# Constant loads at the head of SP's queue, block loads moved next to their use, and the mask moved from slot 28 to slot 10

## The reference

```python
x = x + tanh(g_xattn[0]) * L0_xattn(layernorm(x), ...)
x = x + tanh(g_ffn[0]) * L0_ffn(layernorm(x), ...)          # stage B and the start of stage C
x = x + tanh(g_xattn[1]) * L1_xattn(layernorm(x), ctx, ctx, mask, Wq, bq, ..., Wo, bo)
x = x + tanh(g_ffn[1]) * L1_ffn(layernorm(x), w1, conv_w, conv_b, w2)

# L0_ffn: per-tensor quantised activations, per-row quantised weights, inner width 1408
xq   = act_fake_quant(x, clip_x)                 # scale, clip to -128..127, round
gate = xq @ weight_fake_quant(w_gate).T
up   = xq @ weight_fake_quant(w_up).T
h    = act_fake_quant(silu(gate) * up, clip_down)   # needs the largest |silu(gate)*up| of all tokens
y    = h @ weight_fake_quant(w_down).T
# L1_ffn quantises w1 and w2 to -1, 0, 1 with the mean of their absolute values as scale
```

## Time and profile before

| | us |
|---|---|
| median of 3 runs | 1983.57 (1983.23 to 1985.07) |
| the profiled execution, its own time | 1985.07 |
| its span | 1983.3 |
| stage B in it | about 975 to 1158 |

### The profile page before, as it was taken

The page is one execution under the profiler, slowest core; times in us unless marked ns, Lnnn a source line. Parts: engine busy times, 40 slices in busy tenths (PEclk is TensorE's granted clock), DMA queues, the critical chain, the costliest instruction groups (busy, mean ns, idle before and its releaser), DMA issues.

```text
span 1983.3 us, 24380 instructions
## 1 busy us (share of the span) xinstructions
PE 1599.7 (81%) x9442; PEld 718.8 (36%) x9510; DVE 1743.9 (88%) x2619; ACT 1485.4 (75%) x1098; POOL 616.9 (31%) x480
## 2 busy tenths in 40 slices
PE   6858966698557966785599969999999976888887
PEld 3212211122112211231244426666666632334432
DVE  6899998999999987898598877999998669999997
ACT  4899999999999999999354845554554357767771
POOL 1000000000000000000062236666666446887881
PEclk9999999999999999999799989999999988999998
DMA  5000200020000010000387753333332110432312
GB/s 199 1 0 29 79 11 1 22 75 22 1 1 1 22 54 1 1 11 1 110 312 291 265 172 100 112 112 112 107 100 81 43 37 27 79 61 70 57 43 74
DMA packets 116710, 143.66 MB, mean 72 GB/s; under 512 B 25327, under 2 KB 74607, under 8 KB 116211
## 3 DMA queue, kind: packets, MB, share of 16 engines
q1 hardware_dynamic: 116594, 142.10, 22.9%
HBM read 87.55 MB, written 50.33 MB: 70 GB/s over the span
## 4 chain that ended last, share of the span: by engine, by line
ACT 43%; PE 30%; DVE 19%; issue 4%; POOL 3%; DMA 2%; SPq 0%; DVEq 0%; another core or an unknown queue 0%; POOLq 0%; ACTq 0%
ACT unit L514 39%; PE psum L1647 5%; PE psum L1681 5%; PE psum L1633 3%; DVE hmax_parts L1429 3%; DVE psum L1418 3%; PE psum L1016 3%; PE psum L1010 3%; DVE unit L423 2%; PE psum L1657 2%; PE psum L1674 2%; POOL hidden L1837 1%; PE psum L1666 1%; PE psum L547 1%; DVE hidden_q L1453 1%
## 5 line engine op out<-in xcount | busy, mean ns | idle before, releaser
L514 ACT ACTIVATE unit<-unit 128x4096 f32<-128x4096 f32 x244 | 857.6, 3620 | 0.5 <-DVE unit L423 0.3
L423 DVE TENSOR_SCALAR unit<-feat_proj,text_proj 128x1024 f32<-128x1024 f32 x976 | 667.5, 747 | 67.2 <-PE psum L639 65.2
L639 PE MATMUL psum<-unit,w_pad 128*32 128x512 f32 x3904 | 474.8, 605 | 234.1 <-ACT unit L514 234.1
L639 PEld LDWEIGHTS psum<-unit,w_pad 128*32 128x32 f32 x3904 | 102.5, 109 | 557.3 <-ACT unit L514 398.6
L680 POOL TENSOR_SCALAR red<-red 128x8 f32<-128x8 f32 x4 | 2.0, 510 | 531.5 <-DVE red L321 531.5
L1820 POOL TENSOR_TENSOR h<-h,arow 128x512 f32<-128x512 f32 x104 | 135.7, 1318 | 73.0 <-ACT h L1582 72.8
L1699 PE MATMUL psum<-xq_block,w_q 128*128 128x512 bf16 x489 | 122.8, 391 | 27.5 <-ACT hidden L1601 21.3
L680 POOL TENSOR_SCALAR rstd<-mv 128x8 f32<-128x8 f32 (+1 forms) x5 | 1.7, 336 | 411.7 <-DVE mv L216 411.7
L547 PE MATMUL psum<-xnT,W_sb 128*128 128x512 f32 x256 | 125.2, 617 | 2.1 <-ACT xnT L465 2.1
L1589 ACT ACTIVATE psum<-h,conv_b_sb,conv_w_sb 128x512 f32<-128x512 f32 x112 | 86.2, 779 | 53.6 <-POOL h L1820 46.7
L1734 PE MATMUL psum<-w_q,hidden_q 128*128 128x512 fp8e4 x448 | 104.1, 386 | 20.8 <-ACT hidden_q L1612 12.3
(11 more groups left out here) (255 smaller groups left out, 2790.0 us busy)
## 6 DMA issues: line engine op xcount, KB each, us to landing
h_scratch<-h SPq DMA_DIRECT2D x44, 512.0 KB, 4.4
hin<-h_scratch SPq DMA_DIRECT2D x32, 704.0 KB, 4.7
xin<-in_x SPq DMA_DIRECT2D x8, 1024.0 KB, 6.7
tern_in<-in_w1T SPq DMA_DIRECT2D x16, 512.0 KB, 4.2
tern_in<-in_w2T SPq DMA_DIRECT2D x16, 512.0 KB, 6.8
x<-in_x SPq DMA_DIRECT2D x16, 512.0 KB, 3.7
x_scratch<-x SPq DMA_DIRECT2D x32, 256.0 KB, 2.0
x3in<-x_scratch SPq DMA_DIRECT2D x31, 256.0 KB, 3.1
```

Source lines behind the costliest of these rows:

```text
L423: ins = ve.tensor_scalar(units[:, n % 3, k, :], FP[:, bi % 2, k, :], TP[:, k, n:n + 1], None, ALU.add)
L514: ac.activation(units[:, n % 3], units[:, n % 3], ACT.Tanh).then_inc(unit_tanh, 1)
L639: mm = te.matmul(psum[k * TG:(k + 1) * TG, 3 + 2 * grp + half, :], w_pad[:, k, TG - 1 - tt:2 * TG - 1 - tt], units[:, n % 3, k, half * BAN ...
```

## The change

Four things are changed. The seven constant loads (bq, bo, conv_w, conv_b, the mask, Wq, Wo; 2.4 MB together) are issued ahead of the slot loop instead of one each in slots 18 to 24. The halves of blocks 2 and 3 are loaded in slots i = 2 and 6 of the block before, which is 13, 17, 24 and 28, instead of 5, 9, 16 and 20. The mask and the bias scaling on DVE go from slot 28 to slot 10. The amount of work is the same.

```diff
-    CONST_SLOT, MASK_SLOT = 18, 28
...
-            if n == MASK_SLOT:
+            if n == 10:
                 V.wait_ge(const_c_loaded, NCONST_C)
                 V.wait_ge(gates_done, 2)
                 ve.tensor_scalar(neg_mask[:, :, :], km_u8[:, :, :], 1.0, -NEG, ALU.subtract, ALU.mult)
...
         load_down(1)
-        consts = ((bq_sb[:, :], bq), (bo_row[:, :], bo.broadcast_to([P, D])), (cw_sb[:, :, :], conv_w),
-                  (cb_sb[:, :], conv_b), (km_u8[:, :, :], kmask.rearrange("(t p) k -> p t k", p=P)),
-                  (wq_sb[:, :, :], WqT), (wo_sb[:, :, :], WoT))
+        for dst, src in ((bq_sb[:, :], bq), (bo_row[:, :], bo.broadcast_to([P, D])), (cw_sb[:, :, :], conv_w),
+                         (cb_sb[:, :], conv_b), (km_u8[:, :, :], kmask.rearrange("(t p) k -> p t k", p=P)),
+                         (wq_sb[:, :, :], WqT), (wo_sb[:, :, :], WoT)):
+            sp.dma_start(dst, src).then_inc(const_c_loaded, 16)
         for n in range(NH):
...
             for half in range(2):
-                if o + 2 < NB and i == ROUND_SLOT[half] + 1:
-                    load_block(o + 2, half)
+                if 1 <= o < NB - 1 and i == ROUND_SLOT[half] - 2:
+                    load_block(o + 1, half)
...
-            if CONST_SLOT <= n < CONST_SLOT + len(consts):
-                sp.dma_start(*consts[n - CONST_SLOT]).then_inc(const_c_loaded, 16)
             S.wait_ge(h_done, 2 * n + 1)
```

## The result

The changed kernel takes 1998.32 us (1998.03 to 2000.37), the kernel before 1983.4 (1982.93 to 1985.07) beside it: ratio 1.0079 [1.0066, 1.0091], 14.9 us slower. The forecast was 1993.5, with a range of 1987 to 2000. The profiled execution took 1998.16 us, with a span of 1996.4. Its span is only 13.1 us longer than that of before, because the profiled execution of before was the slowest of its kernel, 1.7 us over the median.

The account below looks back on a forecast made before the run. PE sets the feed-forward stage's pace, but DVE has no spare time in slots preparing the next block. Late loads of slots 13 and 17 (7.4), slot 24 (0.5) and slot 28 with mask (2.0) add 9.9 us to 1983.57: 1993.5, range 1987 to 2000.

Parts of the forecast that it names:

- slot 13's term: DVE's scaling in slot 13 waits for its late block load, landing after 8.3 us: 4.7 us late (1.8 to 5.2).
- slot 28 with the mask: Block in slot 28 3.5 us late, less 1.5 for the mask leaving: 2.0 us (0.8 to 4.2).
- The fall of the clock: PE's idle time from slot 13's wait may lower its granted clock; nothing added, since slot 17's load wait would hide it.
- The second term: DVE's scaling in slot 17 waits for its late block load, landing after 6.6 us: 2.7 us late (1.5 to 4.9).
- Slot 24: Block load with only a store in front, 0 to 0.9 us late: 0.5 us taken (3.4 with 8.8 us landing).
- rival C: A crowded queue: landings of 8.8 us in all four places, +17.7 us, 2001.3; chance 9%.
- Costs of nothing: Mask in slot 10 lies in DVE's wait for PE, cost 0; constants ahead of the loop cost 0, at most some 2 us.
- Rival D: Constants' burst near 985 us delays a part ACT reads in slots 5 to 7: some 2 us, 1995.5; chance 3%.
- Rival A: Quick landings: late block loads land like a lone one, 5.4 us: +4.1 us, 1987.7; chance 8%.
- Rival B: Not slower: DVE's waits vanish in PE's and DVE's lead, only the mask's 1.5 us gain remains: 1982.1; chance 5%.
- PE's lead of 0.6 us: Gate matmuls of slot 16 start 0.6 us after h of slot 14 ends, so longer DVE delays there reach PE.

Follow-up runs that it names:

- the last: Everything but the block loads of the changed kernel, plus PE's product of the weight sums and DVE's use of it one slot later: 1978.06 us, ratio 0.9974 [0.9964, 0.9984].

## Why the prediction was right, and where it fell short

The direction, the place and the kind of wait were as forecast; the size was 9.9 us where 14.9 came, inside the range. That it lay inside is in part luck: slot 13's term alone measured 7.4 us, outside its own bounds of 1.8 to 5.2, and the sum stayed below the range's end because slots 17 and 24 came in far below their upper bounds. Lateness of h against before, with the 0.35 us by which after was ahead added:

| after the step | forecast | measured |
|---|---|---|
| slot 13 | 4.7 | 7.4 |
| slot 17 | 7.4 | 10.2 |
| slot 24 | 7.9 | 10.8 |
| slot 28 with the mask | 9.9 | 14.45 |
| end of stage B | 9.9 | 15.5 |

*Slot 13.* Issue at 1036.0 forecast, 1036.04 measured. The failed term is the landing: "so I take 8.3 us", where it was 10.5. I took it from the block load of 1012.78, "which also had such transfers right ahead", and that reading was wrong: right ahead of that load SP had issued two parts and a store, but no down weight row. I also let the leaving block load of slot 9 count as relief and bounded the landing by 8.8, the worst of the six, a load (1025.62) with no such row right ahead either. Two rows of the windows view after (columns as in the earlier trace rows):

```profile
1025.00:1030.00 5.00, 5.00 (x25) 2.27 (x24) 4.79 (x6) 2.99 (x3) 3.28 (x2) 1.00 1.00 320
1030.00:1035.00 5.00, 5.00 (x27) 2.63 (x26) 4.25 (x5) 2.06 (x2) 3.80 (x2) 1.00 0.92 300
```

and the same time before:

```profile
1025.00:1030.00 5.00, 4.95 (x24) 2.27 (x24) 3.88 (x4) 3.34 (x4) 3.16 (x3) 1.00 1.02 411
```

The second stretch of before stands in the earlier trace rows. Two loads of 1 MB have left slots 5 and 9, but the DMA engines show nearly as busy as they did, 1.00 and 0.92 against 1.02 and 1.04. They move 320 and 300 GB/s instead of 411 and 406; over the ten us that is 0.99 MB less, about the load of slot 9. The rest of the traffic went hardly faster without it: the weight row of slot 11 landed after 8.4 us instead of 8.9, the store behind it after 9.2 instead of 9.7. So the late load came into a queue that was nearly as far behind as before. The run with the weight row moved shows that row's part, 1.8 us of the landing, which then is 8.7 and close to the 8.3 taken; why the rate is lower isn't settled.

*The fall of the clock.* The prediction saw that PE's idle time in slot 16 could bring it and added nothing, because slot 17's wait would hide it. The first half held: 6.67 us idle, then a granted clock of 0.57 (1047 to 1055), gate matmuls of 3.59 us. So did the second: h of slot 17 is 8.4 us late, the block arrives 1.69 us after that. With slot 17's load early the same fall is paid in full, as the run with one late load shows. A cost that is hidden behind another isn't free; it returns when the other is mended.

*Slot 17.* The second term was forecast at 2.7 and is 2.8 (10.2 less 7.4): 1.1 of it the slow matmuls, 1.7 the wait. Landing 6.9, 6.6 taken.

*Slot 24.* 0.5 forecast, 0.52 measured, with a landing of 5.9. With the constants still in slots 18 to 24 it was 2.79: moving them away did help here, and only here.

*Slot 28.* The wait was forecast at 3.5 and is 5.03, again by the landing, 8.1 where 6.6 was taken by likeness to slot 17. The block went in behind a part, and taking the part away brought it to 6.9. Less the mask's 1.5 the term is 3.6 (14.45 less 10.8) where 2.0 was forecast.

*The end.* After slot 28 another 1 us is lost: PE idles 4.89 us in slot 31, and its gate matmuls take 3.22 us. The forecast had no term for it. ACT's wait of 2.88 us for the part that is loaded right behind slot 28's block, which rival C named, came too but costs nothing by itself: it ends at 1120.91, and ACT then idles 2.37 us for PE before the silu of slot 31. Stage C gives little back that is the change's: this trace of after gains 2.0 us there on that of before, but the trace of the constants alone, a kernel as fast as before, gains 1.5.

*Costs of nothing.* The mask in slot 10: right, h of slot 11 comes 0.24 us later relative to the work (0.7 was forecast), h of slot 12 is on time again, and no idle time of an engine follows. The constants: right, 1.0000 [0.9991, 1.0008]; SP's timeline has them from 985.17 to 990.79, so 5.6 us where 5.5 was worked out, and the first store at 990.83. Rival D is out by that run. Rival A (5.4 us landings) is out: no late load of the changed kernel came in under 5.9. Rival B is out: DVE waits, and PE's lead of 0.6 us shortened only PE's own idle time (6.67 against 7.28), while h of slot 14 is late by the whole wait. Rival C, the crowded queue, has come true in slot 13, by more than its 8.8 us, and nearly in slot 28 (8.1).

The Trainium skill, DMA: Bandwidth & Descriptors, section Anatomy of one DMA, has a single transfer's time depend on its bytes alone, an estimated 4.4 us for 1 MB on the GpSimd path. All loads here go through SP's queue, so no run tests that fit on its own path. For SP's queue the traces disagree with both: the same 1 MB took 5.5 to 10.5 us in one execution, by what had been issued ahead of it, and 11.0 in one of the experiments.

## What to carry to other kernels

A load next to its use must be priced with the landing that it will have in that place: who is right ahead in the queue and what the DMA engines do in that stretch, not the landing of a load that was issued elsewhere. In a queue that one engine issues in order, a load is only as early as the last wait ahead of it: moving the one of slot 13 by a slot of 3.46 us moved its issue by 0.85. And an earlier issue can bring it behind a larger transfer, as in slot 24, where a whole slot won in the issue was lost in the landing. Where loads are already 20 us ahead of their use, moving other traffic out of their way is worth nothing (the constants here); look instead for an engine that waits with everyone behind it, as PE did for the weight sums.

## What the hardware showed that was not expected

- DMA engines with a busy share of 0.92 to 1.04 moved between 300 and 411 GB/s in the same stretch of nearly the same program, by which loads were among the traffic: more block loads, more bytes, about the same busy share. The cause isn't settled.
- The same 1 MB load in one execution: 5.5 us at the head of the stage, 5.9 behind a store, 6.9 behind a store and a part in slot 17, 8.1 behind the same two in slot 28, 10.5 behind a weight row, a part and two stores.
- PE's matmuls ran slower after idle times of 4.89, 6.30 and 6.67 us, by 1.3 to 1.7 us for the eight gate matmuls (3.22, 3.60 and 3.59 against 1.89). Ahead of the mean's product PE idled for 3.23 to 4.27 us in every run but the last, and there the outcome varied: the gate and up matmuls behind it took 3.78 us together in the run with everything but the block loads (idle 3.23, clock 1.00), 5.51 in the kernel before (idle 3.58) and 6.67 in the run one slot earlier and ahead of the part (idle 3.23, clock 0.50). So two executions of nearly the same program can differ by almost 3 us there, and the length of the idle time doesn't tell which way it goes. Why is open.
- The mask's first instruction (128x512, uint8 to float32) took 1.16 us in slot 28 of the kernel before, 0.93 in slot 10 and 0.42 in slot 28 behind a late block. In slot 28 before POOL had an instruction running for most of that time (1105.03 to 1106.07), in slot 10 for the first 0.64 us, behind the late block none; that this is the cause is not shown.
